# The last attention's scores as alternating 64-row tiles, in a reordered step

## The reference

```python
q = _split_heads(xn @ Wq)
kv = xn @ Wkv
mem = _split_heads(memories @ Wm)          # ctx_1024, 722 rows
k = jnp.concatenate([k, mem], axis=2)
v = jnp.concatenate([v, mem], axis=2)
dots = jnp.einsum('bhid,bhjd->bhij', q, k) * scale
attn = jax.nn.softmax(dots, axis=-1)
out = jnp.einsum('bhij,bhjd->bhid', attn, v)
return out.transpose(0, 2, 1, 3).reshape(b, n, h * d) @ Wo + bo
```

## Time and profile before

| | |
|---|---|
| median of 3 runs | 1920.87 us (1920.75 to 1921.82) |
| span of the profiled execution, first to last instruction | 1915.0 us |
| median less span | 5.9 us |
| mean granted TensorE clock | 0.935 |
| TensorE busy | 1695.5 us (89%) |
| VectorE busy | 1117.1 us (58%) |
| ScalarE busy | 794.7 us (42%) |
| steps of the last attention, first to last scores | 852.4 to 1493.0 us |

### The profile page before, as it was taken

How to read it: one execution, slowest core, us unless ns; L and a number is a source line. 1 busy time by engine, 2 the same in 40 slices (tenths; PEclk the granted TensorE clock), 3 DMA queues, 4 the chain that set the end, 5 groups by cost and what they waited for, 6 DMA issues and landing times. The chain is left out here.

```text
span 1915.0 us, 31965 instructions
## 1 busy us (share of the span) xinstructions
PE 1695.5 (89%) x11552; PEld 1430.1 (75%) x11552; DVE 1117.1 (58%) x1856; ACT 794.7 (42%) x1416; POOL 142.9 (7%) x189
## 2 busy tenths in 40 slices
PE   6996359999999589889999999999999709999993
PEld 5775359999999289568787878778787609999981
DVE  5765546667677553125555556565557436766765
ACT  2443135555555143124444444344445215445440
POOL 4000310000000301100000000000000040000004
PEclk9998579999999789889999999999999759999997
DMA  9300265655666346241212111121111055665644
GB/s 343 132 9 1 82 231 201 212 202 197 209 208 219 97 176 240 71 115 36 57 29 52 39 47 39 42 53 30 44 23 23 1 202 180 217 213 188 217 144 123
DMA packets 117458, 236.62 MB, mean 124 GB/s; under 512 B 54232, under 2 KB 74840, under 8 KB 102268
## 3 DMA queue, kind: packets, MB, share of 16 engines
q1 hardware_dynamic: 100396, 182.28, 29.9%
q0 software_dynamic: 16976, 53.11, 8.0%
HBM read 187.17 MB, written 48.17 MB: 123 GB/s over the span
## 5 line engine op out<-in xcount | busy, mean ns | idle before, releaser
L955 DVE TENSOR_TENSOR e_lo<-e_raw,e_hi 128x2048 fp32r<-128x2048 f32 x118 | 270.4, 2291 | 129.0 <-ACT e_hi L1018 129.0
L918 PE MATMUL banks<-e_xh,e_hi 128*128 128x256 f32 x1024 | 291.8, 285 | 12.3 <-DVE e_xl L971 7.4
L918 PE MATMUL banks<-e_xh,e_lo 128*128 128x256 f32 x1024 | 291.1, 284 | 0.0
L918 PE MATMUL banks<-e_xl,e_hi 128*128 128x256 f32 x1024 | 291.1, 284 | 0.0
L1600 PE MATMUL banks<-a_wm,a_ch 128*128 128x512 f32 (+1 forms) x768 | 250.1, 407 | 13.5 <-DVE a_cl L1736 13.5
L1018 ACT CAST e_hi<-e_raw 128x2048 fp32r<-128x2048 f32 x118 | 224.7, 1904 | 70.5 <-PE banks L935 28.6
L918 PEld LDWEIGHTS banks<-e_xh,e_hi 128*128 128x128 f32 x1024 | 197.4, 193 | 20.7 <-issue 8.2
L918 PEld LDWEIGHTS banks<-e_xl,e_hi 128*128 128x128 f32 x1024 | 197.3, 193 | 5.6
L918 PEld LDWEIGHTS banks<-e_xh,e_lo 128*128 128x128 f32 x1024 | 197.2, 193 | 0.0
L1634 PE MATMUL banks<-a_kT,a_qD 128*100 128x512 f32 (+1 forms) x768 | 173.9, 362 | 1.9 <-DVE a_kT L1746 1.9
L1752 DVE TENSOR_REDUCE a_nmax<-banks 100x1 f32<-100x822 f32 x128 | 129.5, 1012 | 75.7 <-PE banks L1634 75.7
(11 more groups left out here) (237 smaller groups left out, 2742.4 us busy)
## 6 DMA issues: line engine op xcount, KB each, us to landing
e_raw<-wout SPq DMA_DIRECT2D x50, 1024.0 KB, 4.7
e_raw<-w SPq DMA_DIRECT2D x34, 1024.0 KB
e_raw<-wgate SPq DMA_DIRECT2D x17, 1024.0 KB
e_raw<-wup SPq DMA_DIRECT2D x17, 1024.0 KB, 4.8
a_craw<-ctxT SPq DMA_DIRECT2D x40, 256.0 KB, 2.9
e_xs<-slot_rows SPq DMA_DIRECT2D x18, 512.0 KB
slot_outs<-e_y POOLq DMA_DIRECT2D x16, 512.0 KB, 3.2
slot_rows<-a_zero POOLq DMA_DIRECT2D x15, 512.0 KB, 10.4
```

The lines of the kernel that those rows point to most:

```text
L918: mm = nc.tensor.matmul(ps[:, bank, 0:CAP], w[:, cc, cut], x[:, cc, :], start=t == 0, stop=t == len(terms) - 1)
L955: nc.vector.tensor_tensor(lo[g % 2][i][:], raw[q % RAW][:], hi[g % 2][i][:].bitcast(F32), ALU.subtract)\
```

## The change

The queries are no longer padded: `qD` becomes `q` with the pair's 128 rows, one transfer instead of two, and GpSimd's memsets with SyncE's wait for them go. The scores of both heads are one block: for each of the six products, a 64-row matmul of head 0 (partitions 0 to 63, banks 0 and 1) is followed by one of head 1 (partitions 64 to 127, banks 2 and 3), and one semaphore step stands for both. The block waits for both exponentials of the pair before.

The step is reordered around it. Between the two turns, where the second head's scores stood, there is now one of three things (`between`): the attended product (moved there from before the middle values, in steps without a second group of values or an output), the second group of values (steps 0, 2, 3, 4 with `left >= 1`), or the output (step 1). In the second and third case the attended product stays ahead of the middle values. The last thing in every step is now the turn of head 1. VectorE takes both maxima at the start, then the low keys, both normalisations, the middle values, and the turns with the end values between them; ScalarE takes both exponentials one after the other.

```diff
+    def between(m, left):
+        return "output" if m == 1 else "values" if left >= 1 and m in END else "attended"
-        qD = [k.sb(c, f"a1_qD{u}", [128, 2, 2, T], F32R) for u in range(SLOTS)]
+        q = [k.sb(c, f"a1_q{u}", [128, 2, T], F32R) for u in range(SLOTS)]
...
-                    after(sp, sc, 2 * (IC * b + m - SLOTS + 1))
-                    for two in range(2):
-                        r = slice(64 * two, 64 * two + 64)
-                        sp.dma_start(qD[s][r, :, two, :].bitcast(F32),
-                                     s1.q[:, bass.ds(b, 1), r, m, :].rearrange("n b p t -> p (n b) t"))\
-                            .then_inc(qk_in[s], 16)
+                    after(sp, sc, IC * b + m - SLOTS + 1)
+                    sp.dma_start(q[s][:].bitcast(F32),
+                                 s1.q[:, bass.ds(b, 1), :, m, :].rearrange("n b p t -> p (n b) t"))\
+                        .then_inc(qk_in[s], 16)
-                sp.wait_ge(made, SLOTS)
-            @block.gpsimd
-            def _(pool):
-                for s in range(SLOTS):
-                    pool.memset(qD[s][:].bitcast(U32), 0).then_inc(made, 1)
...
-                def scores(p, m, two):
+                def scores(p, m):
                     s = m % SLOTS
-                    after(pe, ex, 2 * p + two - 1)
+                    after(pe, ex, 2 * p)
                     for f, (first, wide) in enumerate(WIDE):
-                        for t, (q, kk) in enumerate(((0, 0), (0, 1), (1, 0))):
-                            mm = nc.tensor.matmul(ps[0:T, 2 * two + f, 0:wide], qD[s][:, q, two, :],
-                                                  kT[s][:, kk, first:first + wide], start=t == 0, stop=t == 2)
+                        for t, (qn, kk) in enumerate(((0, 0), (0, 1), (1, 0))):
+                            for two in range(2):
+                                r = slice(HD1 * two, HD1 * two + HD1)
+                                mm = nc.tensor.matmul(ps[0:T, 2 * two + f, 0:wide], q[s][r, qn, :],
+                                                      kT[s][r, kk, first:first + wide], start=t == 0, stop=t == 2)
                     mm.then_inc(sc, 1)
...
+                    if what != "attended":
+                        heads()
                     if left >= 1 and m in MIDDLE:
                         values_ahead(b, MIDDLE[m])
                     if exists(p - 1):
                         if ahead:
                             pe.wait_ge(tl, p + 2)
                         turn(p - 1, (m - 1) % IC, 0)
-                    if left >= 0:
-                        scores(p, m, 1)
+                    if what == "attended":
+                        heads()
+                    elif what == "values":
+                        values_ahead(b, END[m])
+                    elif exists(p - 2):
+                        output(b, left)
                     if exists(p - 1):
                         turn(p - 1, (m - 1) % IC, 1)
-                    if left >= 1 and m in END:
-                        values_ahead(b, END[m])
...
                         highest(p, m, 0)
+                        highest(p, m, 1)
                     if left >= (1 if m == IC - 1 else 0):
                         keys(p + 1, (m + 1) % IC)
-                    if exists(p - 1):
-                        normalise(p - 1, (m - 1) % IC, 1)
                     if left >= 0:
                         normalise(p, m, 0)
+                        normalise(p, m, 1)
                     if left >= 1 and m in MIDDLE:
                         evacuate(b + 1, 1 - u, MIDDLE[m], 6)
                     if exists(p - 1):
                         turned(p - 1, (m - 1) % IC, 0)
-                    if left >= 0:
-                        highest(p, m, 1)
+                    if left >= 1 and m in END:
+                        evacuate(b + 1, 1 - u, END[m], 6)
                     if exists(p - 1):
                         turned(p - 1, (m - 1) % IC, 1)
-                    if left >= 1 and m in END:
-                        evacuate(b + 1, 1 - u, END[m], 6)
...
                         exponent(p, m, 0)
-                    if exists(p - 2):
+                        exponent(p, m, 1)
+                    what = between(m, left)
+                    if exists(p - 2) and what != "attended":
                         attended(p - 2, (m - 2) % IC)
...
```

More of the change, by code:

```diff
@@ L1490, in attend @@
         rinv = k.sb(c, "a1_rinv", [T, H1])
-        made = k.sem("a1_const")
         craw_in = [k.sem(f"a1_craw_in{u}") for u in range(3)]
@@ L1662, in step @@
                     if left >= 0:
-                        pe.wait_ge(qk_in[m % SLOTS], 48 * (2 * b + m // SLOTS + 1))
+                        pe.wait_ge(qk_in[m % SLOTS], 32 * (2 * b + m // SLOTS + 1))
                         pe.wait_ge(tl, p + 1)
-                        scores(p, m, 0)
+                        scores(p, m)
                     ahead = left >= (1 if m == IC - 1 else 0)
@@ L1674, in step, with heads @@
                             keys(p + 1, m + 1, u)
-                    if exists(p - 2):
[L1676 to L1679, removed]
+                    what = between(m, left)
+                    def heads():
+                        if exists(p - 2):
+                            if m == 2:
+                                pe.wait_ge(v_in[u], 8 * (b - u) + 16)
+                            attended(p - 2, (m - 2) % IC, u if m >= 2 else 1 - u)
+                    if what != "attended":
+                        heads()
                     if left >= 1 and m in MIDDLE:
@@ L1685, in step, with output @@
                         turn(p - 1, (m - 1) % IC, 0)
-                    if left >= 0:
-                        scores(p, m, 1)
+                    if what == "attended":
[4 more added lines that the diff above has]
+                        output(b, left)
                     if exists(p - 1):
                         turn(p - 1, (m - 1) % IC, 1)
-                    if left >= 1 and m in END:
-                        values_ahead(b, END[m])
[L1692 to L1701, removed]
+                def output(b, left):
+                    pe.wait_ge(ys, IC * b + 2)
+                    if left >= 1:
+                        values_copied(b + 1, MIDDLE[1])
+                    elif type(b) is int:
+                        pe.wait_ge(os_, b)
+                    for j in range(IC):
+                        mm = nc.tensor.matmul(ps[0:T, 6, :], yT[:, j, :], s1.wo[:, j, :],
+                                              start=j == 0, stop=j == IC - 1)
+                    mm.then_inc(od, 1)
                 for n in range(NV):
@@ L1750, in highest @@
                     h = 2 * m + two
-                    dve.wait_ge(sc, 2 * p + two + 1)
+                    dve.wait_ge(sc, p + 1)
                     nc.vector.tensor_reduce(nmax[:, h:h + 1], two_banks(2 * two)[0:T, 0:KEYS], AX, ALU.max, negate=True)\
@@ L1850, in step @@
                         turned(p - 1, (m - 1) % IC, 0)
+                    if exists(p - 2) and what == "attended":
+                        attended(p - 2, (m - 2) % IC)
+                    if what == "values":
+                        evacuate(b + 1, 1 - u, END[m], 6)
+                    if exists(p - 1):
                         turned(p - 1, (m - 1) % IC, 1)
[L1852 to L1855, removed]
                     if m in SPLIT and left >= SPLIT[m][0]:
```

## The result

| | before | after |
|---|---|---|
| median of 12 runs | 1919.52 us (1915.78 to 1921.82) | 1915.65 us (1911.6 to 1919.42) |
| ratio, 95% interval | | 0.998 (0.997 to 0.9989) |
| span of the profiled execution | 1915.0 us | 1913.4 us |
| mean granted TensorE clock | 0.935 | 0.930 |
| TensorE busy | 1695.5 us | 1662.3 us |

What follows compares the result with a forecast made beforehand. TensorE's own work was taken to bound the loop. Terms -44.2 (tiles) + 22.5 (stalls) + 6 (last batch) - 5 (start) = -20.7 us gave a 1894 us span, 1900 median; own range 1886 to 1914, wider range 1878 to 1923.

Steps and rivals of the forecast that it cites:

- Parts 1 and 2: Scores in the attention's steps: side-by-side tiles save 1.12 us, switching tile shape costs 0.33; net 0.79 a step, 44.2 in all.
- Rival A: Scores' block: the two row tiles run one after the other, block 2.24 + 0.33 us; kernel 1963 us; chance 0.08.
- rival B: Scores' block: weight loads are no longer hidden, 0.98 us a step returns; kernel 1953 us; chance 0.04.
- Part 3: Loop: bank 6 used twice with one turn between; stalls of 0.39 us in steps 3 and 4, 0.29 in 0 and 1.
- Part 4: Step 2 of a batch: late additions on VectorE stall TensorE 0.5 us for low keys and 1.4 for bank 6, together 1.9.
- Part 6: Start of the stage: no zeros to wait for and fewer transfers cut TensorE's idle time; 5 us saved, bounds 0 and 6.
- Part 5: Last batch: less work covers the wait for the low keys; steps 7.05 us, 0.9 longer; +6 us in all.
- what follows the last scores I leave as it is: Stretch behind the last batch's last scores: its chain of copies stays, forecast difference 0.
- rival D: Waits are worse: slacks of steps 5 to 7 gone (+6 us), switch at 0.6 (+17); kernel 1923 us; chance 0.12.

Runs made afterwards that it cites:

- end_last: Changed kernel with the second group of values behind the second turn, attended product between the turns in every step but 1; 1905.19 us, 0.9923 of before.
- adds_early: Changed kernel with VectorE's additions of the output no longer behind step 1's split, which moves behind step 2's low keys; 1908.07 us, 0.9945 of before.
- filled: Changed kernel with 16 unread matmuls in TensorE's wait for the low keys, last batch's steps 0, 1, 3 to 6; 1912.03 us, 0.9964 of before.
- all_three: Changed kernel with the edits of `heads_first` (attended product before the first turn, last batch), `adds_early` and `end_last` together; 1897.69 us, 0.9894 of before.
- tail: `all_three` with the very last pair's second exponential and second normalisation behind the copies of the pair before; 1894.42 us, 0.9858 of before.
- order_alone: Changed kernel's order with whole-height matmuls, padded queries, their memsets and two transfers again; 1963.43 us, 1.0232 of before.
- heads_first: Changed kernel with the attended product ahead of the first turn in the last batch and after it; 1910.56 us, 0.9958 of before.

## Why the prediction was right or wrong, point by point

Parts 1 and 2, the tiles: right. Block and borders together are 1.45 us, as forecast: from the start of the turn ahead, 1124.71, to the start of the attended block, 1127.47, less 0.60 for the turn and 0.71 for the keys with the way into the attended block, as they cost before. Steps 5 and 6 fell by 0.79 and 0.83, forecast 0.79. Rival A (one after the other) and rival B (the loads come out) are refuted by the block's rows; B's rule from the Trainium skill (TensorE: Matmul & The Clock Gate, Part 3, The mechanism), that a weight load overlaps only matmuls of another row group, fails here too: in the block, each tile's next load (1125.73 us, 162 ns) lies beside matmuls of both tiles (1125.73 to 1126.12).

Part 3, bank 6: right. Steps 3 and 4 came out 0.1 us longer than forecast, and taking the second group away from there gave 0.3 to 0.5 us back (`end_last`).

Part 4, step 2: right in size, 12.53 for 12.3, and the two waits, 0.54 and 1.23 us, are the 0.5 and 1.4 forecast. The cause is shown for part of it: with the additions early (`adds_early`) the step falls by 0.87 us and the first wait goes, but 1.06 us of the second stay. The split, 0.6 us, then stands in VectorE's list ahead of that copy, so how much of the second wait the late additions cause is not separated.

Part 6, the start: right, 5.2 for 5 us, and 5.7 when put back. The transfer went out 4.5 us earlier where 3.7 were counted, and the clock's slow stretch went with the idle time, which the forecast had as a perhaps.

Part 5, the last batch: this is the step that failed. The waits were sized well: steps without values took 7.05 us where the clock stayed up, as forecast, and steps 1 and 2 took 12.63 and 8.06 against 12.9 and 8.2. But the idle 2.1 us in each of these steps was counted only by its length. In the last batch no term and no rival had the clock, though the clock's 0.50 behind an idle stretch stands in the earlier trace rows. The term of +6 us measured +11.7. The clock is worth 6 us of it in the profiled execution, shown by `filled`; other kernels with the same last batch took up to 67.8 us for it. It also cost 3 us in two of the step 2's. That the waits are the cause there too is likely, since in `adds_early` and `all_three` step 2 waits less and the clock did not fall in the loop; but it did not fall in the loop of `end_last` either, where step 2 is as long as in the changed kernel, so it is not shown. The sentence "what follows the last scores I leave as it is" was wrong too, by 2.9 us. The copy of the previous pair's turn stood behind both exponentials and both normalisations. That the order is a cause is shown by the wait in `tail`; how the 2.9 us divide between it and the clock, whose mean fell from 0.99 to 0.86 in that stretch, is not.

The rest of the gap lies in small waits. The loop came out 7.2 us short of the forecast: 3.0 from the clock, 3.6 from 0.6 us a batch (0.2 of it in step 7, where the second turn starts 1.53 us behind the attended block and not 1.36 as in step 6; that it waits for VectorE's copy, late by the split at the head of the step, is argued only), the remainder in the first batch. Together, 7.2 in the loop, 5.7 in the last batch and 2.9 behind it, less 0.2 at the start, are the 15.6 us between -20.7 and -5.1. The measured time lies between the forecast's 1900 and rival D's 1923, but D is not borne out by that: it had put its price on steps 5 to 7 and on the switch, neither of which paid it but for 0.2 us in step 7, and no rival had the clock. That the kernel came out faster at all is near to luck: the gain is 3.9 us, and the start alone carries more.

What `order_alone` adds: the order that the tiles need is no small item beside them. By itself it costs 44 us, as much as the tiles save in the loop by the forecast. With the tiles in place the forecast had 22.5 + 6 for it; what it missed sits where TensorE is idle.

## What to carry to other kernels

Two heads of 64 rows can go through TensorE side by side for the price of one, if their matmuls alternate and write different banks, as here; going into the tile shape and out of it again cost about a third of a microsecond for each block. A wait that an engine's saving uncovers costs more than its length where TensorE's clock falls behind it. So look for the steps with the least other work, and move work that is needed anyway into the wait. Matmuls that nobody reads kept the clock up as well, but where they were longer than the wait they cost their own time. When two blocks are merged, ask for each bank what stood between its two uses before: that cover goes with the merge.

## What the runs showed of the hardware that was not expected

Two row tiles overlap to a part even without alternation: six 64-row matmuls of one tile and then six of the other took 1.85 us, against 1.30 alternating and 2.31 at whole height.

In the last batch of the changed kernel the granted clock fell from 1.00 to 0.50 four times, for 3.4 us each, with idle stretches of 2.1 us around it and TensorE busy for 47.78 of 62 us. The longest idle stretch, 3.10 us in step 2, was not followed by a fall there, but in `filled` it was. The seven steps of `all_three` ran at full clock throughout, with TensorE busy for 41.72 of 54 us; the same steps ran partly at the lower level in `heads_first` and `tail` (57.9 us for seven). Which idle stretch brings it down is not settled.
